# A transformer layer on one core: batch copies, halved key turns, a reordered opening and a last tile in token halves

## What is computed

```python
xn = layernorm(x)                                # over 1024
q, k, v = xn@Wq.T+bq, xn@Wk.T+bk, xn@Wv.T+bv     # each as [token, 32 heads, 32]
scores = einsum('bshd,bsgd->bshg', q, k) / sqrt(32)   # heads against heads, in one token
scores = where(scores > 0.001, scores, -inf)
ctx = einsum('bshg,bsgd->bshd', softmax(scores), v)
attn = ctx.reshape(.., 1024) @ Wo.T + bo
# int4 weights with a scale for each 128 inputs; inner width 3584
ffn = (silu(xn @ Wg.T) * (xn @ Wu.T)) @ Wd.T
out = x + attn + ffn
```

## Time and profile before

| | us |
|---|---|
| median of 3 runs | 2074.03 |
| range of the runs | 2073.51 to 2074.03 |
| the profiled execution | 2074.31 |
| its span in the trace | 2072.5 |
| TensorE busy | 1997.5 |
| VectorE busy | 1561.4 |
| POOL busy | 1348.1 |
| ScalarE busy | 1232.2 |

### The profile page before, as it was taken

One profiled execution on the slowest core, in us unless ns is written; L12 is line 12 of the kernel. 1 busy time (PEld: TensorE's weight loads), 2 busy tenths in 40 slices (PEclk: granted clock), 3 DMA queues, 4 the chain that ended last, 5 costly groups with the idle time before them and its releaser, 6 DMA issues. The chain is left out here.

```text
span 2072.5 us, 35869 instructions
## 1 busy us (share of the span) xinstructions
PE 1997.5 (96%) x10380; PEld 952.7 (46%) x10380; DVE 1561.4 (75%) x1552; ACT 1232.2 (59%) x1988; POOL 1348.1 (65%) x769
## 2 busy tenths in 40 slices
PE   9999999999998999899999999999999999999986
PEld 5555554554554444334444444444444444444434
DVE  6566667667664300699999999999999999999996
ACT  5577777777774311246666666666665666666652
POOL 1455645545553000069888988888888888898885
PEclk9999999999998999999999999999999999999998
DMA  9576676766767372122122112212221212221226
GB/s 271 133 176 167 157 175 159 164 171 154 173 166 185 92 245 76 32 60 51 46 66 66 46 51 61 71 46 51 53 78 46 51 46 73 58 51 46 63 86 247
DMA packets 397931, 217.95 MB, mean 105 GB/s; under 512 B 335427, under 2 KB 372291, under 8 KB 395846
## 3 DMA queue, kind: packets, MB, share of 16 engines
q1 hardware_dynamic: 397894, 217.46, 39.8%
HBM read 94.73 MB, written 41.94 MB: 66 GB/s over the span
## 5 line engine op out<-in xcount | busy, mean ns | idle before, releaser
L1237 POOL TENSOR_TENSOR acc<-acc,lower 128x1024 f32<-128x1024 f32 x327 | 770.4, 2365 | 162.3 <-ACT lower L950 162.2
L655 PE MATMUL banks<-xt,lower 128*128 128x512 f16 x3584 | 857.1, 379 | 13.5 <-DVE lower L1127 8.7
L950 ACT ACTIVATE lower<-banks,down_scale 128x512 f32<-128x512 f32 x654 | 414.4, 684 | 381.4 <-PE banks L680 295.9
L1127 DVE SCALAR_TENSOR_TENSOR lower<-banks,gate_scale,lower 128x1024 f32<-128x1024 f32 x392 | 479.0, 1278 | 143.4 <-PE banks L655 142.4
L655 PEld LDWEIGHTS banks<-xt,lower 128*128 128x128 f16 x3584 | 343.4, 98 | 458.2 <-DVE lower L1127 74.2
L505 PE MATMUL banks<-wt,xt_tile 128*128 128x512 f16 x2304 | 527.9, 379 | 0.0
L1127 DVE SCALAR_TENSOR_TENSOR lower<-banks,up_scale,lower 128x1024 f32<-128x1024 f32 x392 | 479.2, 1278 | 26.6 <-PE banks L655 23.6
L680 PE MATMUL banks<-lower 128*128 (+1 forms) x1792 | 462.3, 382 | 12.0 <-DVE acc L1180 11.8
L1199 POOL TENSOR_TENSOR stacks<-unit,stacks 128x512 f16<-128x512 f32 x192 | 246.8, 1309 | 295.1 <-ACT stacks L779 295.1
L505 PEld LDWEIGHTS banks<-wt,xt_tile 128*128 (+1 forms) x2304 | 218.4, 98 | 229.9 <-issue 1.1
L680 PEld LDWEIGHTS banks<-lower 128*128 (+1 forms) x1792 | 172.5, 98 | 230.7 <-issue 13.0
(11 more groups left out here) (64 smaller groups left out, 1228.5 us busy)
## 6 DMA issues: line engine op xcount, KB each, us to landing
v_scratch<-stacks SPq DMA_DIRECT2D x16, 1024.0 KB, 3.9
lower<-in_L_ffn_gate_q_dram SPq DMA_DIRECT2D x28, 512.0 KB, 3.6
lower<-in_L_ffn_up_q_dram SPq DMA_DIRECT2D x28, 512.0 KB, 4.4
lower<-in_L_ffn_down_q_dram SPq DMA_DIRECT2D x28, 512.0 KB, 3.9
x_tile<-in_L_attn_x_dram SPq DMA_DIRECT2D x16, 512.0 KB, 3.5
xt_scratch<-xt_tile SPq DMA_DIRECT2D x16, 512.0 KB, 2.9
ctx_scratch<-ctx_parts SPq DMA_DIRECT2D x64, 128.0 KB, 2.1
lower<-ctx_scratch SPq DMA_DIRECT2D x4, 2048.0 KB, 8.8
```

What stands on the lines that cost most here:

```text
L655: last = mm(psum[:, 2 * (slot % 3) + c, :], gu_t[:, mat, g, :], xt[:, (2 * half + c) * CT:(2 * half + c + 1) * CT, part, g, :], start=(par ...
L950: run(down_tmp[:, buffer, c * BANK:(c + 1) * BANK], psum[:, 6 + c, :], ACT.Copy, scale=scale)\
L1127: v.scalar_tensor_tensor(out=acc_of[:, half, :], in0=gu_pair(slot % 3), scalar=scale[:, :, :].rearrange("p t k -> p (t k)")[:, bass.ds(t * ...
L1237: g.tensor_tensor(acc[:, half, ho, :], acc[:, half, ho, :], down_tmp[:, buffer, :], ALU.add).then_inc(down_added, 1)
```

## The change

Three groups of edits. (1) Middle: batches R0, R1 and R3 are copied by VectorE, R2 by ScalarE; the keys are turned in two halves with a semaphore each, the first as soon as unit 2 is split. (2) Opening: the biases come by three DMAs that write one row to 128 partitions, issued behind the loads of w = 10, 13 and 15; bv is put in its order by a copy on POOL between units 1 and 2. The bias matmuls and copies are gone. Quarter w-8 stands ahead of weight w instead of behind it, and the four batches stand behind quarters 17, 19, 21 and 23. (3) The last FFN tile goes by token halves: `LAST_ORDER` has first the 16 gate/up units of half 0, then those of half 1. The hidden part of half 0 is made in that tile on POOL (at units 20 and 26, ScalarE at 23), that of half 1 in the tail on POOL, where VectorE made both. The tail starts with the down units of tile 27 for half 0, and OUT0 to OUT5 lie among the others. The first two residual loads are issued when half 0 has its last unit, the DOWN turn of tile 27 behind them, then the other two.

The diff, cut to its core:

```diff
+        BATCH_AT = {17: 0, 19: 1, 21: 2, 23: 3}
+        BIAS_AT = {10: 0, 13: 1, 15: 2}
@@ def opening
             for w in range(ROWS, 3 * KT):
+                quarter(w - ROWS)
                 weights(w)
-                quarter(w - ROWS)
                 second_x(w)
@@
+        LAST_ORDER = [(GATE, g, 0) for g in range(5)] + [(UP, 0, 0)]
+        for g in range(5, KT):
+            LAST_ORDER += [(GATE, g, 0), (UP, g - 4, 0)]
+        LAST_ORDER += [(UP, g, 0) for g in range(4, KT)]
+        for g in range(KT):
+            LAST_ORDER += [(GATE, g, 1), (UP, g, 1)]
+        def by_halves(t):
+            return isinstance(t, int) and t == NI - 1
+        def unit_of(t, idx):
+            if by_halves(t):
+                return LAST_ORDER[idx]
+            return idx // 16, idx // 2 % 8, idx % 2
@@
-        LEAD = 11
-        TAIL = [(NI - 2, d) for d in range(EARLY, 16)] + [(NI - 1, d) for d in range(LEAD)]
-        for d in range(LEAD, 16):
-            TAIL += [(OUT, d - LEAD), (NI - 1, d)]
-        TAIL += [(OUT, u) for u in range(16 - LEAD, TT)]
+        HALF_OUT, LAST_OUT = 3, 6
+        TAIL = [(NI - 1, d) for d in range(8)] + [(NI - 2, d) for d in range(8, 8 + HALF_OUT)]
+        for n, item in enumerate([(NI - 2, d) for d in range(8 + HALF_OUT, 16)] + [(NI - 1, d) for d in range(8, 16)]):
+            if n % 2 == 0 and n // 2 < LAST_OUT:
+                TAIL.append((OUT, n // 2))
+            TAIL.append(item)
+        TAIL += [(OUT, u) for u in range(LAST_OUT, TT)]
         def by_pool(item):
-            return item[1] % 3 == 1 if item[0] == OUT else item[1] in (1, 3, 6, 9, 11, 14)
+            return item[1] % 3 == 1 if item[0] == OUT else item[1] in (1, 4, 9, 11, 14)
@@
-        SILU_AT = {19: 0, 27: 1}
+        OWN_AT = {20: "h", 26: "l"}
+        OWN_HI_AT = 23
+        def silu_at(t):
+            return {13: 0, 31: 1} if by_halves(t) else {19: 0, 27: 1}
@@ TensorE, batch
-                wait_pos(pe, batch_out[m % 2], j * 2 + m // 2)
+                if m < 2:
+                    wait_pos(pe, batch_out[m], j * (1, 3)[m])
+                else:
+                    pe.wait_ge(batch_out[1], j * 3 + (m - 1))
@@ TensorE, scores
-                    pe.wait_ge(k_turned, j * 16 + 16)
+                    pe.wait_ge(k_turned[0], j * 16 + 16)
+                    pe.wait_ge(k_turned[1], j * 16 + 16)
@@ TensorE, first_quarter
                 project(0, s)
+                if s in BATCH_AT:
+                    pe.wait_ge(w_hi, 3 * KT)
+                    pe.wait_ge(w_lo, 3 * KT)
+                    batch(0, BATCH_AT[s])
@@ ScalarE, tile_2 (VectorE has n != 2)
-                        elif kind == "R" and n % 2 == 0:
+                        elif kind == "R" and n == 2:
                             batch_copy(i, n)
@@ ScalarE, behind the last tile
             for n, (t, d) in enumerate(TAIL_POOL):
-                if n in (1, 3):
-                    hidden_hi(NI - 1, n // 2)
                 down_copy(t, d, TAIL_FROM + n)
+                if n == 2:
+                    hidden_hi(NI - 1, 1)
@@ VectorE, behind the last tile
-            hidden(NI - 1, 0)
-            hidden(NI - 1, 1)
-            dve.wait_ge(down_added, 2 + TAIL_FROM)
             for n, (t, d) in enumerate(TAIL_FAST):
-                if n in (0, 2):
-                    hidden_lo(NI - 1, n // 2)
+                if n == 2:
+                    dve.wait_ge(down_added, 2 + TAIL_FROM)
@@ POOL
             def first_units():
                 for u in range(6):
                     unit_part(0, u)
+                    if u == 1:
+                        pool.wait_ge(bias_loaded[V], 16)
+                        g.tensor_copy(bias_qkv[:, V, :].rearrange("p (d h) -> p d h", h=NH),
+                                      bias_rows.rearrange("p (h d) -> p d h", d=DH)).then_inc(bias_turned, 1)
@@ POOL, last tile and behind it
+                    if idx in OWN_AT and by_halves(t):
+                        (hidden if OWN_AT[idx] == "h" else hidden_lo)(t, 0)
             tiles(pool, tile)
+            pool.wait_ge(gu_added, adds_made(NI, -1))
             for n, (t, d) in enumerate(TAIL_POOL):
+                if n == 2:
+                    hidden(NI - 1, 1)
+                if n == 3:
+                    hidden_lo(NI - 1, 1)
@@ SP, opening
-            for n, b in enumerate((bq, bk, bv)):
-                sp.dma_start(bias_rows[n], b.rearrange("(a n) -> a n", a=1)).then_inc(bias_loaded[n], 16)
...
                 load_w(w)
+                if w in BIAS_AT:
+                    n = BIAS_AT[w]
+                    sp.dma_start((bias_qkv[:, Q, :], bias_qkv[:, K, :], bias_rows)[n],
+                                 (bq, bk, bv)[n].rearrange("(a n) -> a n", a=1).broadcast_to((P, H)))\
+                        .then_inc(bias_loaded[n], 16)
@@ SP, turn_k
-                sp.wait_ge(unit_lo, i * 6 + (2 * K + 2))
...
-                sp.dma_start_transpose(k_turns, stacks[:, K, :, :].rearrange("p x c -> p (x c)"))\
-                    .then_inc(k_turned, 16)
+                for half in range(2):
+                    sp.wait_ge(unit_lo, i * 6 + (2 * K + 1 + half))
+                    anchor(sp)
+                    at = slice(half * (NH // 2), (half + 1) * (NH // 2))
+                    sp.dma_start_transpose(k_turns[:, at, :], stacks[:, K, at, :].rearrange("p x c -> p (x c)"))\
+                        .then_inc(k_turned[half], 16)
@@ SP, behind the last tile
-            turn_q(DOWN, NI - 1)
-            sp.wait_ge(gu_done, units_made(NI, -1))
             for c in range(4):
+                if c == 2:
+                    turn_q(DOWN, NI - 1)
+                if c % 2 == 0:
+                    sp.wait_ge(gu_done, units_made(NI - 1, GU_SLOT[15 + 8 * c]))
                 sp.dma_start(x_res[:, 4 * c:4 * c + 4, :], ...
```

More of the change, by code:

```diff
@@ L169, in build @@
         unit_lo = sem("unit_lo")
-        k_turned = sem("k_turned")
+        k_turned = [sem(f"k_turned{k}") for k in range(2)]
         v_stored = sem("v_stored")
@@ L397, in in_use, with index_of, is_first, firsts_made @@
             return kind == "gu" or not isinstance(t, int) or t >= 2 or (t == 1 and unit >= FIRST_DOWN)
-        def is_first(slot):
+        LAST_ORDER = [(GATE, g, 0) for g in range(5)] + [(UP, 0, 0)]
[10 more added lines that the diff above has]
+            return idx // 16, idx // 2 % 8, idx % 2
+        def index_of(t, mat, g, half):
+            return LAST_ORDER.index((mat, g, half)) if by_halves(t) else 16 * mat + 2 * g + half
+        def is_first(t, slot):
             kind, unit = SLOTS[slot]
-            return kind == "gu" and unit // 2 % 8 == 0
+            return kind == "gu" and unit_of(t, unit)[1] == 0
+        def firsts_made(t, mat, half):
+            return t * 4 + ((2 * half + mat if by_halves(t) else 2 * mat + half) + 1)
         def units_made(t, slot):
@@ L410, in adds_made @@
             before = (0, 28)[t] if isinstance(t, int) and t < 2 else 32 * t - 6
-            return before + sum(in_use(t, n) and not is_first(n) for n in range(slot + 1))
+            return before + sum(in_use(t, n) and not is_first(t, n) for n in range(slot + 1))
         def has_prev(t):
@@ L611, in tile_2 @@
                             head_products(i - 1, n)
[L613 to L618, removed]
             def first_tile():
-                for n in (Q, K, V):
-                    spread_bias(n)
                 opening(weights, lambda: None, first_quarter, lambda w: None)
-                for m in range(4):
-                    batch(0, m)
             walk(pe, first_tile, tile_2)
@@ L639, in pair_free @@
                     before -= 3
-                if is_first(before):
-                    unit = SLOTS[before][1]
-                    pe.wait_ge(gu_first, tile_of * 4 + (2 * (unit // 16) + unit % 2 + 1))
+                if is_first(tile_of, before):
+                    mat, _, half = unit_of(tile_of, SLOTS[before][1])
+                    pe.wait_ge(gu_first, firsts_made(tile_of, mat, half))
                 else:
@@ L646, in gate_up @@
             def gate_up(t, idx):
-                mat, g, half = idx // 16, idx // 2 % 8, idx % 2
+                mat, g, half = unit_of(t, idx)
                 slot = GU_SLOT[idx]
-                if idx in (0, 16):
+                if g == half == 0:
                     pe.wait_ge(q_ready[mat], 16 * t + 16)
@@ L914, in first_group @@
                 acc_of, scale = (g_acc, gate_scale) if mat == GATE else (u_acc, up_scale)
-                act.wait_ge(gu_done, units_made(t, GU_SLOT[16 * mat + half]))
+                slot = GU_SLOT[index_of(t, mat, 0, half)]
+                act.wait_ge(gu_done, units_made(t, slot))
                 if mat == UP:
@@ L954, in tile @@
                 for idx in range(32):
-                    if idx in (0, 1, 16, 17):
-                        first_group(t, idx // 16, idx % 2)
+                    mat, g, half = unit_of(t, idx)
+                    if g == 0:
+                        first_group(t, mat, half)
```

(8 more changed lines are left out.)

66 lines of the change are left out of this document (20 added, 46 removed).

## The result

The changed kernel takes 2035.56 us, the median of five runs (2033.97 to 2036.75), against 2074.03 (2073.51 to 2074.89) for the kernel before beside it: ratio 0.9814, 95% interval 0.9803 to 0.9825. The forecast was 2034.3. The profiled execution has a span of 2033.8 us, 38.7 less than before; 40.0 were forecast.

What follows compares the result with a forecast made beforehand. TensorE, busy 1997.5 of 2072.5 us, was taken as the bound, with gains from its idle time; 14.7 (middle) + 11.0 (opening) + 14.3 (tail) = 40.0 us off 2074.31 gave 2034.3 us, own range 2028 to 2041.

Steps and rivals of the forecast that it cites:

- Middle, 14.7: Middle attention tiles: 13 batch waits of 1.43 us vanish, a new V0 wait of 0.3 us appears; 14.7 us gained.
- Keys in halves, 0: Key turns in attention tiles: halves give more slack before S0 but no time; 0 us.
- Rival 5: Key turns: a half takes as long as the whole, so S0 waits in 14 tiles; slower, 2091 us; 3%.
- Opening, 11.0: Start to first scores: bias matmuls removed and batches spread; 6.3 + 1.3 + 3.4 = 11.0 us gained.
- weight 8 at 19.7: Opening: weight 8 is transposed at 19.7 us instead of 26.04, 6.3 us gained.
- 1.3 + 3.4: Opening: quarter 0 falls into weight 8's wait, 1.3 us; spread batches shorten the stretch before the first scores, 3.4 us.
- Last tile, 0.5 lost: Last FFN tile: eight sums directly follow the one they need, each some 0.1 us later; 0.5 us lost.
- Tail, 14.3 with the last tile: Behind the last gate/up unit: POOL without a gap, then nine output tiles, set the end; 14.3 us gained.
- Rival 3: Tail: TensorE and not POOL bounds it; 20 us gained there, 2029 us in all; 12%.
- Rivals 1, 2 and 4: 1: VectorE's R0 copy delays V0, 2047, 15%; 2: opening load-bound, 2042, 12%; 4: last tile's order gains nothing, 2049, 3%.
- Rival 2: Opening stays bound by loads: broadcasts of 4 us leave 3 us of its gain; 2042 us; 12%.

Runs made afterwards that it cites:

- part_twice2: The changed kernel with one more POOL subtraction of 0.67 us ahead of the first low part of the probabilities of each tile; 2041.9 us, one run.
- keys_whole: The changed kernel with the keys turned in one piece again instead of in halves; 2038.22 us, ratio 0.9829.
- wo_first: The changed kernel with keys turned whole, but in tile 15 the first two Wo rows issued ahead of the key turn; 2036.09 us, ratio 0.9820.
- pool_less: The changed kernel with the sum of down unit 11 moved from POOL to VectorE, in tiles 26 and 27; 2033.77 us, ratio 0.9812.
- pool_less2: The changed kernel with the sums of down units 11 and 14 moved from POOL to VectorE, in tiles 26 and 27; 2033.61 us, ratio 0.9811.
- turn_late: The changed kernel with the turn of x of tile 1 issued behind the last value rows; 2033.69 us, ratio 0.9811.
- bias_early: The changed kernel with the three bias broadcasts issued ahead of the turn of x, right behind the first eight rows; 2036.75 us, ratio 0.9826.

## Why the prediction was right, point by point

**Middle, 14.7: right.** The waits for copies are gone, V0 waits 0.28 us, the 13 tiles give 15.5 us, 1.2 each. That nothing else covers the path from POOL's part to V0 is shown by `part_twice2`.

**Keys in halves, 0: right in the tiles, wrong at their end.** The prediction named what stands behind the key turn on SP, but followed it only in a tile that repeats. In tile 15 Wo rows stand there; 3.3 us (`keys_whole`, `wo_first`). Rival 5 didn't occur: both halves issue in 5.98 us, where one whole took 4.85, and S0 never waits for them.

**Opening, 11.0: mis-sized, 6.2 measured.** Of its three parts the last two were right: from weight 23 to the first scores 14.7 us pass (57.12 to 71.82), before 19.4 (58.61 to 78.04), and 1.3 + 3.4 were forecast. The step that failed is weight 8 at 19.7. It took the turn's issue from the row of an empty queue, 2.05 us, and let x of tile 1 and weight 8 follow the turn at 1.25 us each; behind the Wq rows the issue was 6.02, nothing could be queued meanwhile, and DMA moved only 199 GB/s from 14 to 18 us. In all profiles with this opening weight 8 comes 5.6 to 5.9 us behind the end of that issue, which is what the rows of before had shown as well. That is 1.9 us. The other 3.0 lie between weight 8 and weight 23, which the prediction let run without gaps. It had priced a broadcast at 1.25 us and one costs 1.18, but it let the value loads start at 32 us. They start at 34 as before, because, as I read it, the loads that went out late at 16.45 had used up that lead: from 14 to 20 us DMA moved 1 MB less than it would have at the 410 GB/s of 10 to 12 us, by estimate 2.4 us. Then the turn of tile 1's x holds SP another 10.03 us. The 6.2 us themselves are those of one execution; the six profiles with this opening give 5.0 to 7.3.

**Last tile, 0.5 lost: 1.2 measured** over the whole FFN, 1.1 of it in the last tile: from its first down unit to its 16th TensorE takes 40.25 us (1943.50 to 1983.75), before 39.17 (1967.68 to 2006.85). Eight sums were to come 0.1 us later each; instead the loss sits mainly behind the five gate units that stand in a row at the tile's start, at two new waits for VectorE, behind which the units start 0.42 and 0.43 us later than in the usual rhythm:

```profile
1949.96 1.02 PE L677 MATMUL banks<-xt,lower 128*128 128x512 f16 x4 [0.26 <-DVE lower L1143]
1951.26 1.04 PE L677 MATMUL banks<-xt,lower 128*128 128x512 f16 x4 [0.27 <-DVE lower L1143]
```

**Tail, 14.3 with the last tile: right in mechanism and size.** POOL was to be through with output tile 7 36.2 us behind the start of the last gate/up matmul (2044.6 against 2008.4); it was after 35.1 (2020.36 against 1985.3). Nine output tiles leave from there without a pause. `pool_less` shows that POOL was the bound, and also that it was so only by 2.4 us; `pool_less2` shows how near VectorE is. Rival 3, that TensorE and not POOL is the bound, falls with them.

**Rivals 1, 2 and 4** didn't occur as such. Rival 2, loads that bound the opening, had the right place, but its cause was to be a slow broadcast; what held the loads was the issue of the turns.

## What to carry to other kernels

The price of an issue that turns data depends on what is queued ahead of it: read it from a row with a full queue if it will meet one, and count every load behind it on that engine. An edit that earns nothing in the repeating tile is to be followed once more through the last one, where other work stands behind it in the same queue. When a stage is bound by one engine, move one piece at a time, and count in the trace how many pieces an edit moves: here one number in a list moved two, and of 4.7 us of relief only 2.4 came through before another chain took over. And where one profile of a stage is read, look at others with the same code: here the opening differs by 2.3 us among them.

## What I had not expected of the hardware

- The issue of a turn of x occupies SP for 2.05 us behind an empty queue, 6.02 behind the rows of Wq, 9.56 with three broadcasts more, and 10.03 among the value rows. There its end moves less than its start: from 39.49 to 49.52 us in the changed kernel, 41.01 to 48.49 in `pool_less2`, and 43.43 to 48.89 before the change.
- A broadcast of a 4 KB row to 128 partitions, 512 KB written, costs 1.18 us, no more than a plain load of that size; value rows, loaded in pieces of 128 KB, come at 234 to 244 GB/s in the full slices of the two traces.
- In executions with the same code up to that point TensorE's granted clock from 22 to 28 us is 1.00 (the changed kernel, `wo_first`, `part_twice2`, `pool_less`) or 0.72 to 0.77 (`turn_late`, `pool_less2`, `keys_whole`), and the length of the wait ahead of it doesn't decide which: 2.18, 2.27, 2.22 and 1.95 us in the first, 2.33, 2.17 and 2.01 in the others. After 4.77 us of idleness (`bias_early`) it is 0.50, that is the lower level, 1.2 GHz. A gap can cost more than its length, and a single profile of an opening is uncertain by some 2 us.
